# Head and tail of the scan stage: one conv on TensorE, zeros beside the last scans, and another order of the last batch's steps

## The reference

```python
z = layernorm(x)                                    # the gate, transposed per batch
xin = in_proj_w @ ctx                               # 256 channels
u = silu(causal_conv4(xin, conv_w) + conv_b)
dt, Bm, Cm = split(x_proj_w @ u)
delta = softplus(dt_proj_w @ dt + dt_proj_b);  A = -exp(A_log)
state = state * exp(delta * A) + (delta * u) * Bm   # 16 states, 256 steps
y = (sum(state * Cm) + D * u) * silu(z)
x1 = x + y
xr = layernorm(x1)
gate, expert = top_k(softmax(xr @ Wg), 2)
pos = running count of rows per expert              # over tokens, both choices
rows with pos < 320 go to slot expert * 320 + pos
out = x1 + sum over k of gate * (relu(row @ w1) @ w2)
```

## Time and profile before

| | |
|---|---|
| runs, us | 292.55, 294.06, 295.63 |
| median, us | 294.06 |
| profiled execution, us | 292.54 |
| its span, first to last instruction, us | 290.7 |
| PE, DVE, POOL, ACT busy, share of the span | 83%, 76%, 77%, 60% |
| mean granted clock of PE | 0.909 |

### The profile page before, as it was taken

The page is one execution under the profiler, slowest core; times in us unless marked ns, Lnnn a source line. Parts: engine busy times, 40 slices in busy tenths (PEclk is TensorE's granted clock), DMA queues, the critical chain, the costliest instruction groups (busy, mean ns, idle before and its releaser), DMA issues.

```text
span 290.7 us, 4966 instructions
## 1 busy us (share of the span) xinstructions
PE 242.3 (83%) x1534; PEld 220.6 (76%) x1534; DVE 221.0 (76%) x367; ACT 175.3 (60%) x386; POOL 224.5 (77%) x180
## 2 busy tenths in 40 slices
PE   8957696596957496677898999999999999999990
PEld 7746474375845285556697898999999999999980
DVE  1799999799899999999945575848585757576710
ACT  1889657948996776669017736475655647464500
POOL 1769779879996999999951948878887878787761
PEclk9999979988999957585579999999999999999996
DMA  6569640053002804042035355365555554655120
GB/s 160 226 193 329 185 171 0 2 193 135 0 3 91 272 0 182 2 157 98 0 108 200 110 156 191 122 217 193 185 190 204 182 220 177 225 178 179 35 61 23
DMA packets 15073, 40.38 MB, mean 139 GB/s; under 512 B 2922, under 2 KB 9900, under 8 KB 12112
## 3 DMA queue, kind: packets, MB, share of 16 engines
q1 hardware_dynamic: 11792, 33.15, 33.9%
q0 software_dynamic: 2816, 6.32, 6.3%
q10 hardware_dynamic: 448, 0.70, 0.9%
HBM read 32.72 MB, written 8.49 MB: 142 GB/s over the span
## 4 chain that ended last, share of the span: by engine, by line
PE 39%; DVE 5%; issue 5%; POOL 3%; DMA 2%; ACT 0%; POOLq 0%; DVEq 0%
PE ps L1004 10%; PE ps L1006 10%; PE ps L1005 10%; DVE h L1227 2%; PE ps L1013 2%; DVE hc L1239 2%; PE ps L828 1%; PE ps L742 1%; POOL out L458 1%; PE ps L1020 1%; POOL so_far L449 1%; PE ps L1042 1%; DMA so_far<-out,dst 1%; DMA out<-eo,dst 1%; POOL w2lo L439 1%
## 5 line engine op out<-in xcount | busy, mean ns | idle before, releaser
L352 POOL TENSOR_TENSOR dbu<-du,bsb 128x1024 f32<-128x1024 f32 x31 | 73.6, 2392 | 2.8 <-ACT bsb L532 1.6
L546 ACT ACTIVATE ps<-delta,anegs 128x255 f32<-128x255 f32 x128 | 53.0, 462 | 12.6 <-DVE h L1220 9.3
L1411 DVE SCALAR_TENSOR_TENSOR htlo<-ps,hthi 128x320 fp32r<-128x320 f32 x64 | 30.8, 488 | 34.6 <-ACT hthi L709 26.3
L806 PE MATMUL ps<-stack,sels 64*128 64x256 f32 x64 | 18.0, 371 | 36.6 <-DVE hc L1239 33.0
L828 PE MATMUL ps<-cst,hc 128*128 128x128 f32 x256 | 45.1, 334 | 0.5 <-DVE hc L1239 0.5
L806 PEld LDWEIGHTS ps<-stack,sels 64*128 64x128 f32 x64 | 11.5, 225 | 44.3 <-issue 43.9
L439 POOL TENSOR_TENSOR w2lo<-w2raw,w2hi 128x512 fp32r<-128x512 f32 x30 | 38.7, 1318 | 6.1 <-ACT w2hi L700 6.0
L449 POOL DMA_INDIRECT so_far<-out,dst x24 | 33.1, 1380 | 12.8 <-issue 5.5
L1220 DVE TENSOR_TENSOR_SCAN h<-ps,dbu 128x1024 f32<-128x1024 f32 x18 | 41.1, 2283 | 0.6 <-issue 0.3
L828 PEld LDWEIGHTS ps<-cst,hc 128*128 128x128 f32 x256 | 36.5, 172 | 5.1 <-issue 1.8
L709 ACT ACTIVATE hthi<-ps 128x320 fp32r<-128x320 f32 x64 | 27.8, 438 | 18.6 <-PE ps L1006 14.5
(11 more groups left out here) (175 smaller groups left out, 526.7 us busy)
## 6 DMA issues: line engine op xcount, KB each, us to landing
w1raw<-in_w SPq DMA_DIRECT2D x8, 1024.0 KB
w2raw<-in_w SPq DMA_DIRECT2D x8, 1024.0 KB
bsb<-b_rows SPq DMA_DIRECT2D x7, 1024.0 KB, 7.2
expert_rows<-fill SPq DMA_DIRECT2D x1, 2580.0 KB, 16.0
xe<-expert_rows SPq DMA_DIRECT2D x8, 258.0 KB
out<-x SPq DMA_DIRECT2D x4, 256.0 KB, 5.2
xnat<-in_x SPq DMA_DIRECT2D x1, 768.0 KB, 7.2
xe<-expert_rows SPq DMA_DIRECT2D x8, 64.5 KB
```

What stands on the lines that cost most here:

```text
L352: nc.gpsimd.tensor_tensor(dbu[j % DRING][:], du[:, :, None, cols(b)].to_broadcast([P, EC, 2, L]), bsb[b % 2][:, None, 2 * p:2 * p + 2, :]. ...
L546: ins = nc.scalar.activation(decays(g % SLOTS_DA)[:, c, i * L + 1:(i + 1) * L], delta[:, c, b * L + 1:(b + 1) * L], ACT.Exp, scale=anegs[: ...
L1411: nc.vector.scalar_tensor_tensor(out=htlo[:, f, :], in0=ps[:, f % 4, 0:CAP], scalar=0.0, in1=hthi[:, f, :].bitcast(F32), op0=ALU.max, op1= ...
```

## The change

In the head, the conv of the second chunk goes from DVE to PE: POOL makes four diagonal matrices of its taps from the identity, ACT copies the projection to SBUF, and PE adds four shifted matmuls. The identity is loaded by itself on ACT's queue, dts on SP's. The negation of anegs goes to POOL, the memset of xe to DVE's start, and ACT makes anegs and sels behind `decay_exps(0)`. In the scan stage PE adds four matmuls of zeros to y behind the add_state of steps 26 to 29. In the tail the counts of batches 0 to 2 for the last batch are made ahead of its logits, in a bank of their own; nmx and the variance's EPS go to DVE; ACT scales and copies row tile by row tile, and makes the second choice's rows and the weights behind xthi; `take` goes tile by tile; half of expert 0's w1lo goes from POOL to DVE behind xtlo. Fillers are redistributed. The diff, cut where lines only repeat (a few added semaphores are left out):

```diff
+diag = hc[1][:].rearrange("p c n t -> p (c n) t")
...
+def places(b):
+    bank = DABANK if b == B - 1 else BBANK
+    return ps[:, bank, 0:BT * NE].rearrange("p (t e) -> p t e", e=NE)
...
+    sp.dma_start(dts[:], dt_small).then_inc(s["dts_in"], 16)
     sp.dma_start(xps[:], xproj_t).then_inc(s["xps_in"], 16)
     sp.dma_start(xnat[:, tiles_of(0), :], x[:, tiles_of(0), :]).then_inc(s["x_in0"], 16)
...
-    sp.dma_start(cst[:], consts).then_inc(s["small_in"], 16)
+    sp.dma_start(cst[:, P:NCONST], consts[:, P:NCONST]).then_inc(s["small_in"], 16)
...
+    pool.wait_ge(s["ch_in"], 16)
+    pool.wait_ge(s["ident_in"], 16)
+    for k in range(TAPS):
+        ins = nc.gpsimd.tensor_scalar(diag[:, k, 0:P], ident, ch[:, 1, CONVW + TAPS - 1 - k:CONVW + TAPS - k], None,
+                                      ALU.mult)
+    ins.then_inc(s["diag_done"], 1)
     pool.wait_ge(s["inp_in"], 16)
     pool.wait_ge(s["cw_in"], 16)
     nc.gpsimd.tensor_tensor(cwb[:], cwb[:], inps[:, None, :].to_broadcast([P, TAPS, DI]), ALU.mult
                             ).then_inc(s["cw_done"], 1)
+    pool.wait_ge(s["a_exp"], 1)
+    nc.gpsimd.tensor_scalar(anegs[:], anegs[:], -1.0, None, ALU.mult).then_inc(s["a_neg"], 1)
     pool.wait_ge(s["small_in"], 32)
     z_rstd(1, tiles_of(0))
...
-    for m in range(WP):
+    for m in range(WP // 2):
...
         nc.gpsimd.tensor_tensor(w1lo[:, :, fs], w1raw[:, :, fs], w1hi[:, :, fs].bitcast(F32),
                                 ALU.subtract).then_inc(s["w1lo_done"], 1)
     for j in tiles_range(B - 2):
         send(j)
-    row_rstd(B - 1)
+    pool.wait_ge(s["ln_eps"], B)
+    nc.gpsimd.tensor_tensor(rx[:, tiles_of(B - 1)], vx[:, tiles_of(B - 1)], nhalf[:, tiles_of(B - 1)], ALU.pow
+                            ).then_inc(s["ln_rstd"], 1)
     pool.wait_ge(s["xe_in"], 32)
...
-    act.dma_start(dts[:], dt_small).then_inc(s["dts_in"], 16)
+    act.dma_start(ident, consts[:, 0:P]).then_inc(s["ident_in"], 16)
...
+    act.wait_ge(s["xe0_psum"], EC)
+    nc.scalar.activation(conv0[:, 1, :], ps[:, CBANK, 0:L], ACT.Copy).then_inc(s["xe0_copied"], 1)
     act.wait_ge(s["wdt_psum"], 1)
...
-    for c in range(EC):
-        act.wait_ge(s["cv_done"], c + 1)
-        nc.scalar.activation(u[:, c, cols(0)], conv0[:, c, :], ACT.Silu, bias=ch[:, c, CB:CB + 1]
-                             ).then_inc(s["u_done"], 1)
+    act.wait_ge(s["cv_done"], 1)
+    nc.scalar.activation(u[:, 0, cols(0)], conv0[:, 0, :], ACT.Silu, bias=ch[:, 0, CB:CB + 1]
+                         ).then_inc(s["u_done"], 1)
+    act.wait_ge(s["conv0_psum"], 1)
+    nc.scalar.activation(u[:, 1, cols(0)], ps[:, BBANK, 0:L], ACT.Silu, bias=ch[:, 1, CB:CB + 1]
+                         ).then_inc(s["u_done"], 1)
     nc.scalar.preload_act_table_set(EXP_SET)
+    decay_exps(0, V0BANK)
     nc.scalar.activation(anegs[:], ch[:, :, ALOG:ALOG + DS], ACT.Exp).then_inc(s["a_exp"], 1)
     act.wait_ge(s["sel_in"], 16)
     nc.scalar.activation(sels[:], brow[0:XPC, 0:BC], ACT.Copy).then_inc(s["sel_done"], 1)
-    decay_exps(0, V0BANK)
     logs(0)
     b_copy(0, BBANK)
...
     x1_turned(B - 1)
-    row_scales(B - 1)
     act.wait_ge(s["ln_scale"], B)
-    for j in tiles_range(B - 1):
+    for t in range(BT):
+        j = (B - 1) * BT + t
         nc.scalar.activation(xrow[:, j, 0, 0:DM], x1[:, j, :], ACT.Identity,
                              bias=nmx[:, j:j + 1], scale=rx[:, j:j + 1]).then_inc(s["row_done"], 1)
-    for t in range(BT):
         act.wait_ge(s["row_done"], t + 1)
-        nc.scalar.activation(rowhi[:, t, :], xrow[:, (B - 1) * BT + t, 0, 0:DM], ACT.Copy
+        nc.scalar.activation(rowhi[:, t, :], xrow[:, j, 0, 0:DM], ACT.Copy
                              ).then_inc(s["rowhi_done"], 1)
+    nc.scalar.activation(nrx[:, tiles_of(B - 1)], rx[:, tiles_of(B - 1)], ACT.Copy, scale=-1.0
+                         ).then_inc(s["ln_neg"], 1)
+    act.wait_ge(s["ln_neg"], B)
     top_exp(B - 1)
-    for j in tiles_range(B - 1):
+    def second_row(j):
         nc.scalar.activation(xrow[:, j, 1, 0:DM], x1[:, j, :], ACT.Identity,
                              bias=nmx[:, j:j + 1], scale=rx[:, j:j + 1]).then_inc(s["xn_done"], 1)
-    weigh(B - 1)
...
+    second_row(T // P - BT)
+    weigh(B - 1)
+    second_row(T // P - 1)
     expert(0, True, False)
...
+    def add_zeros(n):
+        for i in range(n):
+            nc.tensor.matmul(y[:, i % BT, 0:P], fill[:, 0:P], onesf[:], start=False, stop=False,
+                             skip_group_check=True)
...
-    def counts(b):
-        pe.wait_ge(s["oh_done"], b + 1)
-        before = ps[:, BBANK, 0:BT * NE].rearrange("p (t e) -> p t e", e=NE)
+    def counts_so_far(b):
+        before = places(b)
         nc.tensor.matmul(before, onesf[0:1, :], cst[0:1, CBASE:CBASE + BT * NE].rearrange("p (t e) -> p t e", e=NE),
                          start=True, stop=False, skip_group_check=True)
+        for k in range(TOPK):
+            for j in range(b * BT):
+                nc.tensor.matmul(before, ones[:], oh[:, j:j + 1, k, :].to_broadcast([P, BT, NE]),
+                                 start=False, stop=False, skip_group_check=True)
+    def counts(b):
+        pe.wait_ge(s["oh_done"], b + 1)
+        before = places(b)
+        if b < B - 1:
+            counts_so_far(b)
         for k in range(TOPK):
             last = nc.tensor.matmul(before, tri[:], oh[:, tiles_of(b), k, :], start=False, stop=False,
                                     skip_group_check=True)
             for t in range(1, BT):
                 last = nc.tensor.matmul(before[:, t:BT, :], ones[:], oh[:, b * BT:(b + 1) * BT - t, k, :],
                                         start=False, stop=False, skip_group_check=True)
-            for j in range(b * BT):
-                last = nc.tensor.matmul(before, ones[:], oh[:, j:j + 1, k, :].to_broadcast([P, BT, NE]),
-                                        start=False, stop=False, skip_group_check=True)
         last.then_inc(s["pos_psum"], 1)
 
     keep_clock(6, V0BANK)
...
-    keep_clock(2, BBANK)
...
         ins = nc.tensor.matmul(ps[:, YBANK, k * DI:(k + 1) * DI], dts[:, DI + k * P:DI + (k + 1) * P],
                                dts[:, 0:DI], start=(k == 0), stop=True, skip_group_check=True)
     ins.then_inc(s["wdt_psum"], 1)
-    keep_clock(6, BBANK)
+    keep_clock(1, V0BANK)
+    pe.wait_ge(s["xe0_copied"], 1)
+    pe.wait_ge(s["diag_done"], 1)
+    for k in range(TAPS):
+        ins = nc.tensor.matmul(ps[:, BBANK, k:L], diag[:, k, 0:P], conv0[:, 1, 0:L - k], start=(k == 0),
+                               stop=(k == TAPS - 1))
+    ins.then_inc(s["conv0_psum"], 1)
+    keep_clock(2, V0BANK)
     pe.wait_ge(s["wdt_done"], 1)
     for k in range(EC):
...
         add_state(g).then_inc(s["ysum_done"], 1)
+        if b == B - 1 and p in (2, 3, 4, 5):
+            if p == 2:
+                pe.wait_ge(s["fill_made"], 1)
+            add_zeros(4)
...
 
     pe.wait_ge(s["scan_done"], SLOTS_DA + STEPS)
-    keep_clock(4, DABANK)
+    keep_clock(4, DABANK + 1)
     pe.wait_ge(s["gate_done"], B)
     turn(zst[:, tiles_of(B - 1), :], False, True).then_inc(s["xt_psum"], 1)
-    keep_clock(3, DABANK)
+    pe.wait_ge(s["oh_done"], B - 1)
+    counts_so_far(B - 1)
+    keep_clock(2, DABANK + 1)
     logits(B - 1)
-    keep_clock(4, DABANK)
+    keep_clock(4, DABANK + 1)
     counts(B - 1)
+    keep_clock(2, DABANK + 1)
     pe.wait_ge(s["xe_zeroed"], 1)
...
-    def take(part, c, last):
-        for t in range(BT):
-            ins = nc.tensor.matmul(ps[:, 6 + c, 0:CAP], part[:, t, c * P:(c + 1) * P], takes[:, t, :],
-                                   start=False, stop=(last and t == BT - 1), skip_group_check=True)
-        return ins
-    pe.wait_ge(s["takes_done"], BT)
-    pe.wait_ge(s["rowhi_done"], BT)
-    for c in range(KC):
-        take(rowhi, c, False)
-    pe.wait_ge(s["rowlo_done"], BT)
-    for c in range(KC):
-        take(rowlo, c, True).then_inc(s["xet_psum"], 1)
-    keep_clock(3, DABANK)
+    def take(part, t, c, last):
+        return nc.tensor.matmul(ps[:, 6 + c, 0:CAP], part[:, t, c * P:(c + 1) * P], takes[:, t, :],
+                                start=False, stop=last, skip_group_check=True)
+    for t in range(BT):
+        pe.wait_ge(s["takes_done"], t + 1)
+        pe.wait_ge(s["rowhi_done"], t + 1)
+        for c in range(KC):
+            take(rowhi, t, c, False)
+    for t in range(BT):
+        pe.wait_ge(s["rowlo_done"], t + 1)
+        for c in range(KC):
+            ins = take(rowlo, t, c, t == BT - 1)
+            if t == BT - 1:
+                ins.then_inc(s["xet_psum"], 1)
+    keep_clock(3, DABANK + 1)
...
+    nc.vector.memset(xe[EROWS[2]:P, 2, :], 0.0).then_inc(s["xe_zeroed"], 1)
     dve.wait_ge(s["ch_in"], 16)
-    dve.wait_ge(s["xe0_psum"], EC)
-    for k, c, steps in ((0, 0, 0), (0, 1, 0), (1, 0, 1), (2, 0, 3), (1, 1, 2), (3, 0, 4), (2, 1, 5), (3, 1, 6)):
-        bank = (WBANK, CBANK)[c]
-        tap = ch[:, c, CONVW + TAPS - 1 - k:CONVW + TAPS - k]
```

(22 more changed lines are left out.)

11 lines of the change are left out of this document (7 added, 4 removed).

## The result

The changed kernel takes 298.29 us in the median of four executions (297.19 to 299.12), the kernel before 293.31 beside it (292.11 to 295.63). The ratio is 1.0163, 95% interval 1.0123 to 1.0203: slower by over 1%, and outside the range of the prediction. The profiled executions give the same picture: 297.46 with a span of 295.4 against 292.54 with 290.7, so 4.7 us of the span are to be found. All ratios here leave out executions over 1.5% above the fastest of their kernel (four of twelve in run 11, five of twelve in run 13, one of eight in run 9, one of the kernel before); with them, the ratios of the medians in runs 11, 13 and 9 would be 1.0095, 1.0061 and 0.9918.

A forecast was written before the change was run, and what follows sets the result against it. DVE paces the scan stage and PE the expert stage, so gains come at the joints. 0.4 - 0.1 + 2.2 - 1.3 = 1.2 us faster, predicting 292.8 us, range 290.3 to 295.0.

The forecast's parts named there:

- Head, +0.4: Up to the first scan: the conv on PE gains 0, the Abs staying near 11.6; moving xe's memset gains 0.4.
- the prediction's own lower bound of 1.0: Head: four diagonals on POOL take 1.0 to 2.0; an identity 1 us later loses up to 1, carried as -1.0 to +0.2.
- The gain of 0.4 by the memset: Head: xe's memset no longer stands between dbu0's end (17.70) and the first scan (18.11), a sure gain of 0.4.
- POOL's chain at no cost: Head: POOL's small copies end 2.4 later, at 17.5, yet dbu1 still ends at 19.9, ahead of the second scan.
- Zeros: Beside the last scans: zeros keep the clock full, so the last sums take 2.0 instead of 3.67, gaining 1.65.
- 1.00 from 126 on: A sign of being right: the granted clock stays at 1.00 from about 126 on.
- The cost of 0.1 at the logits: Scan stage: zeros ahead of batch 2's logits make them end at 132.6, so DVE waits 0.1.
- rival (b): Zeros meet the half clock at step 26 and DVE waits 2.0 longer for logits; -1.2, about 295.3; chance 0.10.
- Tail, +2.2 for the start of the expert: Last scan to first expert: its matmul starts at about 155.5 instead of 157.72, gain 2.2.
- The w2lo stall, 1.3: Expert 0's second product: POOL's work slides 1.7 against a slack of 0.39, so PE waits 1.3, paid once.
- Rival (d): Head: the diagonals come late, gain 0.2 instead of 1.2, 293.8; chance 0.18 shared with another case.
- the prediction's own signs of being wrong: DVE waiting over 0.3 for logits in step 27; taps waiting for diag; w2lo ready in time; late w1 load stalling turn_rows(1).

The follow-up runs named there:

- run 11: The changed kernel with more fillers ahead of wdt and the taps and the negation of anegs on DVE; 1.0064 to the kernel before.
- run 13: The kernel before with ten fillers in PE's idle stretch ahead of the first cast of C; 1.0003 to the kernel before.
- run 9: The tail's part alone, zeros only in steps 28 and 29, so_far set ahead of the last sends, memset of xe ahead of DVE's first conv operation; 0.9915 to before.
- run 4: The changed kernel with more fillers in the head, two ahead of wdt and four instead of one ahead of the taps; 1.0131 to the kernel before.
- run 12: The kernel before with only the negation of anegs moved to POOL, and its Exp and the copy of sels later on ACT; 0.9999 to before.
- run 2: The kernel before with the tail's part of the change alone, zeros included; 1.0005 to the kernel before.
- run 7: The tail's part alone with POOL's memset of so_far moved ahead of the last sends; 0.9992 to the kernel before.
- run 8: The tail's part alone with ten zeros each in steps 28 and 29 instead of eight in 26 to 29; 0.9990 to the kernel before.
- run 10: The whole change, diagonals on ACT, more head fillers, negation on DVE, zeros only in steps 28 and 29, so_far set early; 0.9983 to the kernel before.
- run 5: The changed kernel with the negation of anegs moved from POOL to DVE; 1.0111 to the kernel before.
- run 14: The changed kernel with ten fillers in PE's idle stretch ahead of the first cast of C; 1.0163 to the kernel before.

## Why the prediction was wrong

**Head, +0.4: the term that failed. It was -3.9, of which 3.2 stood at the first scan.** The prediction gave PE's chain 0.25 for each tap instruction, from the earlier trace rows, and it took 0.47. The row read had 12 fillers ahead of it, and the change takes most of these away. The same trace held the other price a little earlier: instructions of the same size, in the projection, at 2.07 for four, 0.52 each. PE in the kernel before:

```profile
3.75 2.07 PE L881 MATMUL ps<-ctxs,inps 128*128 128x256 f32 x4
...
6.26 1.13 PE L886 MATMUL ps<-dts 8*128 8x256 f32 x4
7.32 1.60 PE L742 MATMUL ps<-onesf 128*128 128x128 f32 x12
```

From the start of the taps on, taps, fillers and first_dt all grow at the slow pace; run 4 puts the price at 2.4, and the range had no case for it. The diagonals came to 8.48 where 7.2 was assumed: 2.38 for four, against 2.0 as the upper bound, and the identity at 6.1 where 5 was named. Their 1.2 is a little past the prediction's own lower bound of 1.0. The gain of 0.4 by the memset is real: the first scan follows dbu0 0.03 behind its end in the change (21.35 behind 20.09 + 1.23), where 0.41 lay between the earlier trace rows.

**POOL's chain at no cost: wrong.** It was said to end at 17.5 against 16.66. It ended at 22.4, because it starts behind the late Abs, and because its durations came from rows in which DVE was idle or read PSUM. Price 0.6 at the second scan in the change; run 12 shows that with an early head the step would have held (0.28 of wait, no change of the time).

**Steps 0 to 3, not in the prediction.** A hole in PE's work of about 3 us was there before and is there after. Whether the clock falls behind it differs between profiled executions even where the head is the same (not in the kernel before, but in runs 2, 7 and 8), and a fall costs between 0.1 (run 7) and 1.4 (run 10).

**Zeros: one size right, the way to it partly luck.** 1.65 was forecast for the last sums and 1.71 measured. But the granted clock was not 1.00 from 126 on: it was 0.50 to 136 and again from 144 to 146, add_state(28) took 1.97, and the clock was back in time for the last sums, as it was not in runs 5, 11 and 14. The cost of 0.1 at the logits was 0.9: rival (b)'s mechanism came in, at less than half its price, since add_state(26) ran partly at the half clock (1.50). Run 8 shows that zeros in steps 28 and 29 do as well for the last sums.

**Tail, +2.2 for the start of the expert: right.** 155.58 for 155.5 in run 2, with the steps 0.46 late; in the change 1.71 + 0.87 = 2.58 beside steps that were 0.9 late. **The w2lo stall, 1.3: right in kind.** 1.05 measured, ended by POOL. Run 7 takes it away, but in its profile what that wins is lost again by the end, 0.6 of it in waits at the next expert.

**The sum** had its four terms as 0.4, -0.1, 2.2 and -1.3. Measured: about -3.9 and -1.4 for the head and for the falls of the clock over the steps to 27 (5.29 in all), -0.9, 2.58 and -1.05. Rival (d), late diagonals at 1.0, came in with 1.2; none held slow taps, since PE's cost was taken from a row at the full pace. Two of the prediction's own signs of being wrong were there: the taps waited for the diagonals, and DVE waited 0.81 for the logits.

## What to carry to other kernels

Before work is moved to an engine, list what that engine did in the stretch ahead of it: a duration read behind fillers or behind an idle neighbour holds only with the same company. An operation that takes the place of a parallel one must be costed as a chain, with the landing of every load it needs. And where a change has a good and a bad half, mend and time them apart: here the tail, once mended, was worth 0.9%, and the head hid it. Last, one profiled execution is a sample: where the clock falls in some executions only, a difference of 1 us between two profiles need not be the edit's.
